# Sliding-window attention and two transformer layers: score products of the layers in blocks of 64 queries by 192 keys, a new order of steps, and a regrouped preparation of weights in the first stage

## The reference

```python
# attention: 16 heads of 64, windows of 64 keys
xn = x / max(norm(x), 1e-12) * 16 * gamma
q, k, v = split(xn @ W_qkv)
p = softmax(where(0 <= distance <= 64, q @ k.T / 8, -1e9))   # a block of 64 queries sees 128 keys
out = (p @ v) * sigmoid(xn @ W_gates + b_gates) @ W_out
# two layers: 8 heads of 64, windows of 128 keys
h = shift_token(x); q, k, v = split(h @ wqkv)
q, k = rotary_xpos(l2norm(q) * qs, l2norm(k) * ks)           # q is later scaled by 8
p = softmax(where(0 <= distance <= 128, q @ k.T, -max))      # a block of 128 queries sees 256 keys
x = x + (p @ v) @ wo
h = layernorm(shift_token(x)) * lg + lb
x = x + (a * gelu(g)) @ w2 + b2          # a, g = split(h @ w1 + b1)
```

## Time and profile before

| | before |
|---|---|
| median of 3 runs | 2063.93 us (2059.63 to 2064.92) |
| profiled execution | 2062.13 us, span 2060.3 us |
| PE / DVE / ACT / POOL busy | 92 / 64 / 68 / 47 % of the span |
| mean granted PE clock | 0.986 |

### The profile page before, as it was taken

How to read it: one execution, slowest core, us unless ns; L and a number is a source line. 1 busy time by engine, 2 the same in 40 slices (tenths; PEclk the granted TensorE clock), 3 DMA queues, 4 the chain that set the end, 5 groups by cost and what they waited for, 6 DMA issues and landing times.

```text
span 2060.3 us, 42560 instructions
## 1 busy us (share of the span) xinstructions
PE 1899.8 (92%) x15184; PEld 1575.3 (76%) x15184; DVE 1324.1 (64%) x4117; ACT 1400.8 (68%) x3933; POOL 959.0 (47%) x1311
## 2 busy tenths in 40 slices
PE   5999999999999789999999999997999999999998
PEld 3777787777777668778788787795877878878777
DVE  4543544444443467777778777775777877877775
ACT  4886977778678465775766757756576575675763
POOL 1532442334234463654736526545264562664732
PEclk9999999999999899999999999998999999999999
DMA  3231322313225411010110110304101011010110
GB/s 126 86 101 43 97 82 78 96 58 89 82 75 161 149 39 36 14 42 11 45 45 12 44 42 15 103 7 158 33 29 52 21 45 55 16 47 22 34 35 26
DMA packets 121493, 121.10 MB, mean 59 GB/s; under 512 B 27188, under 2 KB 100804, under 8 KB 121284
## 3 DMA queue, kind: packets, MB, share of 16 engines
q1 hardware_dynamic: 118116, 112.10, 17.0%
q10 hardware_dynamic: 3168, 6.29, 0.9%
HBM read 72.72 MB, written 37.25 MB: 53 GB/s over the span
## 4 chain that ended last, share of the span: by engine, by line
PE 32%; DVE 19%; ACT 9%; issue 2%; POOL 2%; SPq 1%; DMA 1%; DVEq 0%; ACTq 0%; POOLq 0%
PE f_bank L1352 11%; PE f_scores L1492 4%; ACT f_prob L1567 4%; PE f_scores L1430 4%; DVE f_u L1720 4%; PE f_bank L1478 4%; PE f_bank L1438 3%; DVE f_gu L1717 2%; PE f_o_bank L1453 2%; ACT f_u L1587 2%; DVE y_tok L1703 2%; PE f_bank L1403 2%; DVE y_tok L1709 1%; POOL f_prob L1305 1%; DVE f_sin_part L1623 1%
## 5 line engine op out<-in xcount | busy, mean ns | idle before, releaser
L1305 POOL TENSOR_SCALAR f_prob<-f_prob,f_row_inv 128x256 f32<-128x256 f32 x512 | 263.1, 533 | 331.0 <-DVE f_row_inv L1663 331.0
L568 POOL TENSOR_SCALAR a_prob<-a_prob,a_row_inv,a_gate 128x128 f32<-128x128 f32 x512 | 224.6, 455 | 409.8 <-DVE a_row_inv L898 409.8
L1352 PE MATMUL f_bank<-weights,f_actT 128*128 128x512 f32 x1152 | 305.6, 410 | 1.6 <-DVE f_actT L1606 1.6
L1478 PE MATMUL f_bank<-f_hT,f_w 128*128 128x256 f32 x2112 | 276.5, 286 | 7.7 <-DVE f_gu L1717 7.7
L1478 PEld LDWEIGHTS f_bank<-f_hT,f_w 128*128 128x128 f32 x2112 | 262.1, 190 | 14.3 <-DVE f_gu L1717 10.8
L1567 ACT ACTIVATE f_prob<-f_scores,f_neg_max 128x256 f32<-128x256 f32 x512 | 235.9, 488 | 41.8 <-DVE f_neg_max L1655 40.8
L1352 PEld LDWEIGHTS f_bank<-weights,f_actT 128*128 128x128 f32 x1152 | 211.2, 193 | 51.2 <-ACT f_probT L1514 5.1
L1281 POOL TENSOR_TENSOR f_norm<-f_norm,f_minus_half 128x16 f32<-128x16 f32 x64 | 197.5, 3085 | 24.8 <-DVE f_norm L1615 22.4
L1655 DVE CUSTOM_DVE_ANT_0 f_scores<-f_scores,f_mask 128x256 f32<-128x256 f32 x512 | 199.8, 455 | 13.5 <-PE f_scores L1430 13.4
L1587 ACT ACTIVATE f_u<-f_gu 128x256 fp32r<-128x256 f32 x192 | 80.2, 418 | 180.8 <-DVE f_gu L1717 180.8
L797 ACT ACTIVATE a_prob<-a_scores,a_neg_max 128x128 f32<-128x128 f32 x512 | 179.5, 390 | 30.2 <-DVE a_neg_max L889 28.9
(11 more groups left out here) (128 smaller groups left out, 3844.2 us busy)
## 6 DMA issues: line engine op xcount, KB each, us to landing
split_weights<-a_hi_lo SPq DMA_DIRECT2D x16, 512.0 KB, 2.8
x_next<-states SPq DMA_DIRECT2D x32, 256.0 KB, 3.1
tables<-scaled_tables SPq DMA_DIRECT2D x16, 512.0 KB, 6.0
f_x<-states SPq DMA_DIRECT2D x16, 512.0 KB, 5.2
split_weights<-a_hi_lo SPq DMA_DIRECT2D x12, 682.0 KB, 4.0
weights<-split_weights ACTq DMA_DIRECT2D x6, 1024.0 KB, 9.7
f_w<-split_weights SPq DMA_DIRECT2D x4, 1280.0 KB, 9.9
a_x_tok<-in_x SPq DMA_DIRECT2D x8, 512.0 KB, 4.4
```

Of the source, the lines that this page charges most:

```text
L568: last = nc.gpsimd.tensor_scalar(part, part, row_inv[:, a % 2, head, t:t + 1], gate[:, half, t, h:h + 1], ALU.mult, ALU.mult)
L1305: last = nc.gpsimd.tensor_scalar(part, part, row_inv[:, a % 2, head, t:t + 1], 1.0, ALU.mult, ALU.mult)
L1352: last = nc.tensor.matmul(out, lhs(c, a), rhs(c, b), start=(i == 0), stop=(i == len(order) - 1))
L1478: mm = nc.tensor.matmul(out[:, which * PART:(which + 1) * PART], w1[:, wp, c, col:col + P], hT[:, hp, c, columns_of(a // FH)], start=(i == ...
```

## The change

- The layers' score products take 64 queries by 192 keys instead of 128 by 256. Corners that no product writes are cleared once in PSUM. Since the masking then must not change sign, the sign goes into the query tables and the mask.
- `ORDER` is a new list. Among the changes: `transpose_x` stands ahead of the first `softmax`, `load_tables` ahead of `load_others`, `project_o` 1 behind `up` 0, `add_attended` right before `out` 0.
- First stage: x is loaded first; the pieces of weights are cut by groups of heads (both halves of the features in one piece), have a staging place each (the last one shares), and three of the nine splits stand in the first iteration's list `opening`. PE waits for each split only where it is used.
- The squares (`rms_sum`) go; the mean of squares after the norm is computed from the variance (two small DVE instructions). The scaled x goes to a tile of its own, so that `load_x` waits for the scaling and the store, no longer for the transposes.

The diff, cut to its core:

```diff
-        before = [("load_x", e), ("norm_stats", e), ("norm_apply", e), ("rms_sum", e), ("rms_scale", e), ("split", 0), ("rms_apply", e),
-                  ("split", 1), ("transpose_x", e), ("split", 2), ("split", 3), ("split", 4), ("gates", e), ("project_qk", a0), ("gates_back", e), ("split", 5),
-                  ("project_qk", a0 + 1), ("split", 6), ("project_qk", a0 + 2), ("split", 7), ("project_qk", a0 + 3), ("split", 8)]
+        before = [("load_x", e), ("norm_stats", e), ("rms_scale", e), ("norm_apply", e), ("split", 0), ("rms_apply", e), ("split", 1),
+                  ("transpose_x", e), ("split", 2), ("project_qk", a0), ("project_qk", a0 + 1), ("gates", e), ("split", 3), ("project_qk", a0 + 2),
+                  ("gates_back", e), ("split", 4), ("project_qk", a0 + 3), ("split", 5)]
+        opening = list(steps)
+        for n, step in ((6, ("softmax", 0)), (7, ("scores", 1)), (8, ("softmax", 2))):
+            opening.insert(opening.index(step) + 1, ("split", n))
...
+        stages = [raw[:], halves[:, 0], halves[:, 1], y_stage, table_stage, scaled_stage, late_q[:, 0], late_q[:, 1], y_stage]
+        pieces = [(w_gates.rearrange("(c p) n -> p c n", p=P), wgate, slice(0, A_HEADS))]
+        for group in range(A_GROUPS):
+            for n, (place, first) in enumerate(((wqk, 0), (wqk, A_INNER), (wv, 0))):
+                cols, place_cols = (slice(c0 + group * GC, c0 + (group + 1) * GC) for c0 in (n * A_INNER, first))
+                pieces.append((w_qkv[:, cols].rearrange("(c p) n -> p c n", p=P), place, place_cols))
...
+        SPLIT_OF_V, SPLIT_OF_QK, SPLIT_OF_OUT = (3, 6), (2, 7), (7, 8)
...
-                    sp.wait_ge(filled.sem, filled.past(it, ("transpose_x", h - 1), CT - 1) if h else filled.upto(it, -1))
+                    sp.wait_ge(x_ready.sem, x_ready.past(it, ("rms_apply", h - 1)) if h else x_ready.upto(it, -1))
+                    sp.wait_ge(normed_stored.sem, normed_stored.past(it, ("norm_apply", h - 1)) if h else normed_stored.upto(it, -1))
...
+            def load_piece(i):
+                sp.dma_start(stage_of(i), pieces[i][0]).then_inc(staged[i], 16)
+
             load_x(None, HALVES - 1)
-            for i, (src, _, _) in enumerate(pieces):
-                if i == 3:
-                    store_normed(None, HALVES - 1)
-                if i >= 3:
-                    sp.wait_ge(stage_emptied, i - 2)
-                sp.dma_start(stage_of(i), src).then_inc(staged[i % 3], 16)
+            sp.dma_start(ident[:], identity).then_inc(consts_loaded, 16)
+            sp.dma_start(gamma_row[:], gamma.unsqueeze(0).broadcast_to([P, D])).then_inc(consts_loaded, 16)
+            for i in (0, 1, 2):
+                load_piece(i)
+            sp.dma_start(bgate[:], b_gates.unsqueeze(1), allow_slow_non_contiguous=True).then_inc(consts_loaded, 16)
+            sp.dma_start(mask[:], masks.rearrange("s p k -> p s k")).then_inc(consts_loaded, 16)
+            for i in (3, 4):
+                load_piece(i)
+            store_normed(None, HALVES - 1)
+            for i in (5, 6, 7):
+                load_piece(i)
+            sp.wait_ge(stage_emptied, 4)
+            load_piece(8)
             sp.wait_ge(zero_rows_ready, 1)
             sp.dma_start(states[:, 0, :], zero_rows[:]).then_inc(zero_rows_stored, 16)
             sp.wait_ge(zero_rows_stored, 16)
-            sp.wait_ge(stage_emptied, len(pieces))
+            sp.wait_ge(stage_emptied, 1)
...
-            pe.wait_ge(stage_emptied, len(pieces))
...
+                    if a == a0:
+                        pe.wait_ge(stage_emptied, SPLIT_OF_QK[0] + 1)
+                    project_qk(None, a)
...
+                        if it == 0 and a == PAIRS:
+                            pe.wait_ge(stage_emptied, SPLIT_OF_QK[1] + 1)
...
-                    nc.scalar.activation(square[:], x_tok[:, t, :], ACT.Square, accum_out=sumsq[:, t:t + 1]).then_inc(squared.sem, 1)
...
-                dve.wait_ge(squared.sem, squared.past(it, ("rms_sum", h), TILES - 1))
-                nc.vector.tensor_scalar(rms[:], sumsq[:], 1e-24, 1.0 / D, ALU.max, ALU.mult).then_inc(ms_ready.sem, 1)
+                dve.wait_ge(var_ready.sem, var_ready.past(it, ("norm_stats", h)))
+                nc.vector.reciprocal(rms[:], spread[:]).then_inc(spread_inverted.sem, 1)
+                dve.wait_ge(spread_inverted.sem, spread_inverted.past(it, ("rms_scale", h)))
+                nc.vector.scalar_tensor_tensor(out=rms[:], in0=mean_var[:, :, 1], scalar=1e-24 / D * 1e-5, in1=rms[:], op0=ALU.max,
+                                               op1=ALU.mult).then_inc(ms_ready.sem, 1)
...
-                dve.wait_ge(normed_stored.sem, normed_stored.past(it, ("norm_apply", h)))
+                dve.wait_ge(x_normed.sem, x_normed.past(it, ("norm_apply", h)))
+                if it is not None:
+                    dve.wait_ge(filled.sem, filled.past(it, ("transpose_x", h - 1), CT - 1) if h else filled.upto(it, -1))
                 for t in range(TILES):
-                    last = nc.vector.scalar_tensor_tensor(out=x_tok[:, t, :], in0=x_tok[:, t, :], scalar=rms[:, t:t + 1], in1=gamma_row[:],
+                    last = nc.vector.scalar_tensor_tensor(out=x_scaled[:, t, :], in0=x_tok[:, t, :], scalar=rms[:, t:t + 1], in1=gamma_row[:],
...
-ORDER = [("scores", 0), ("scores", 1), ("softmax", 0), ("softmax", 1), ("weigh", 0), ("weigh", 1), ("transpose_x", 0), ("load_x", 0),
-         ("scores", 2), ("transpose", 0), ("softmax", 2), ("scores", 3), ("weigh", 2), ("weigh", 3), ("load_x1", 0), ("load_others", 0),
-         ("transpose", 1), ("softmax", 3), ("load_tables", 0), ("project_qk", 0), ("rope", 0), ("scores", 4), ("values", 0), ("values", 1),
-         ("take_o", 0), ("transpose", 2), ("project_qk", 1), ("softmax", 4), ("scores", 5), ("weigh", 4), ("transpose", 3), ("rope_sum", 0),
-         ("project_qk", 2), ("values", 2), ("softmax", 5), ("scores", 6), ("weigh", 5), ("values", 3), ("rope", 1), ("take_o", 1),
-         ("transpose", 4), ("scores", 7), ("softmax", 6), ("transpose_qk", 0), ("weigh", 6), ("project_qk", 3), ("shift_keys", 0),
-         ("project_o", 0), ("rope_sum", 1), ("weigh", 7), ("transpose", 5), ("values", 4), ("values", 5), ("softmax", 7), ("take_o", 2),
-         ("rope", 2), ("shift_front", 0), ("transpose", 6), ("project_v", 0), ("ln_stats", 0), ("transpose_qk", 1), ("transpose", 7),
-         ("ln_apply", 0), ("values", 6), ("values", 7), ("take_o", 3), ("project_v", 2), ("transpose_h", 0), ("project_o", 1), ("rope_sum", 2),
-         ("up", 0), ("shift_back", 0), ("up", 1), ("up", 2), ("ln_stats", 1), ("project_v", 1), ("ln_apply", 1), ("down", 0), ("project_v", 3),
-         ("up", 3), ("rope", 3), ("x1_bias", 0), ("down", 1), ("down", 2), ("transpose_h", 1), ("load_wqkv", 0), ("up", 4), ("up", 5),
-         ("down", 3), ("add_attended", 0), ("up", 6), ("up", 7), ("up", 8), ("up", 9), ("rope_sum", 3), ("down", 4), ("transpose_qk", 2),
-         ("down", 5), ("up", 10), ("down", 6), ("up", 11), ("down", 7), ("down", 8), ("transpose_qk", 3), ("out", 0), ("down", 9), ("down", 10),
-         ("down", 11), ("out", 1)]
+ORDER = [("scores", 0), ("transpose_x", 0), ("softmax", 0), ("scores", 1), ("weigh", 0), ("load_x1", 0), ("weigh", 1), ("softmax", 1),
+         ("scores", 2), ("transpose", 0), ("scores", 3), ("weigh", 2), ("softmax", 2), ("load_tables", 0), ("transpose", 1), ("softmax", 3),
+         ("values", 0), ("weigh", 3), ("project_qk", 0), ("values", 1), ("rope", 0), ("load_x", 0), ("scores", 4), ("take_o", 0),
+         ("transpose", 2), ("project_qk", 1), ("scores", 5), ("weigh", 4), ("softmax", 4), ("rope_sum", 0), ("load_others", 0), ("transpose", 3),
+         ("values", 2), ("scores", 6), ("weigh", 5), ("softmax", 5), ("project_qk", 2), ("rope", 1), ("values", 3), ("take_o", 1), ("scores", 7),
+         ("transpose", 4), ("softmax", 6), ("weigh", 6), ("project_qk", 3), ("project_o", 0), ("rope_sum", 1), ("weigh", 7), ("transpose", 5),
+         ("values", 4), ("softmax", 7), ("values", 5), ("take_o", 2), ("transpose", 6), ("project_v", 0), ("transpose_qk", 0),
+         ("shift_front", 0), ("values", 6), ("transpose", 7), ("ln_stats", 0), ("shift_keys", 0), ("ln_apply", 0), ("transpose_qk", 1),
+         ("rope", 2), ("transpose_h", 0), ("values", 7), ("take_o", 3), ("project_v", 2), ("rope_sum", 2), ("up", 0), ("project_o", 1),
+         ("up", 1), ("up", 2), ("project_v", 1), ("shift_back", 0), ("down", 0), ("down", 1), ("ln_stats", 1), ("ln_apply", 1), ("down", 2),
+         ("up", 3), ("project_v", 3), ("rope", 3), ("transpose_h", 1), ("up", 4), ("up", 5), ("down", 3), ("up", 6), ("x1_bias", 0), ("up", 7),
+         ("up", 8), ("down", 4), ("rope_sum", 3), ("down", 5), ("down", 6), ("load_wqkv", 0), ("transpose_qk", 2), ("up", 9), ("up", 10),
+         ("down", 7), ("up", 11), ("down", 8), ("down", 9), ("transpose_qk", 3), ("add_attended", 0), ("out", 0), ("down", 10), ("down", 11),
+         ("out", 1)]
...
```

(24 more changed lines are left out.)

125 lines of the change are left out of this document (65 added, 60 removed).

## The result

The change makes the kernel slower. Its median is 2072.5 us (2071.0 to 2075.3) against 2064.0 (2059.6 to 2064.9) of the kernel before: ratio 1.0047, 95% interval 1.0037 to 1.0057 (taken over the single runs; the two medians by themselves give 1.0041). The forecast was 2029, the upper end of its range 2052.

A forecast was written before the change was run, and what follows sets the result against it. PE, busy 1899.8 of 2060.3 us, was taken as the bound, except in chunk openings. Terms -12.8 - 13.3 - 7.4 - 2 + 0.9 = -34.6 us gave 2027.5, forecast as 2029 for the median; range 2000 to 2052.

The forecast's parts named there:

- Part 1: Layers' score products in 64 by 192 blocks: a step falls from 1.07 to 0.84 to 0.86 us, saving 27 us of PE.
- (c): Rival, layers' scores: quadrants don't overlap at 192 columns, 0.43 us a step more, 2095 us in all; chance 0.04.
- (d): Rival, layers' scores: more records cost time of their own and eat the 0.21 us a step, 2043 us; chance 0.03.
- Part 2: New order in each layer chunk: longer opening, shorter scores and fewer POOL waits give -0.8 us a chunk, -12.8 us in all.
- 0.5 us more: Chunk openings: the longer chain swallows the saving of its four score steps and costs this much more a chunk.
- Behind the opening PE is again the one that others follow: Rest of each chunk after the opening: PE sets the pace, so four shorter score steps save 0.85 us.
- -0.85 a chunk: Score steps behind each chunk's opening: four steps save 0.21 us each.
- -0.45: POOL's waits outside the openings: 0.5 us a chunk should nearly vanish, saving 0.45 us.
- Rival (b): Chunk openings: PE's granted clock falls behind the longer wait, +24 us, 2053 us in all; chance 0.10.
- Part 3: Weight reload between layers: tables issued ahead of the weights remove PE's 10.59 us stall and slow clock, -13.3 us.
- Part 4: Program start: x loaded first brings first scores at 33 us, 9.4 earlier; less 2 us for splits on ACT, -7.4 us.
- Part 5: Squares and the rest: removing ACT's squares gives -2 us, DVE's clears of four PSUM tiles cost +0.9 us.

The follow-up runs named there:

- e11: e3 with ten added identity transposes between scores 1 and 2 and five before each head's first transposes, holding the clock; 2046.3 us, ratio 0.9919.
- e4: The changed kernel with 24 unused identity transposes added between scores 1 and 2 of every chunk, holding the clock; 2060.1 us, ratio 0.9978.
- e3: The changed kernel with one step moved back: transpose_x behind softmax 1, as in the old list; 2053.6 us, ratio 0.9952.
- e13: The changed kernel with one small ACT exponential ahead of each chunk's two copies, so the table load comes early; 2072.7 us, ratio 1.0045.
- e5: The kernel before with ten identity transposes added between scores 1 and 2 and five before each head's first transposes, holding the clock; 2062.3 us, ratio 0.9993.
- e8: e6 with half of POOL's division in the layers left out; 2034.2 us, ratio 0.9856.
- e6: e1 with the same added transposes as e5, holding the clock; 2062.6 us, ratio 0.9993 against the kernel before.
- e14: e12 with the old scores, in blocks of 128 queries by 256 keys; 2046.1 us, ratio 0.9919.
- e1: The kernel before with only the 64 by 192 score blocks, the flipped sign and the clears; 2070.1 us, ratio 1.0038.
- e15: The kernel before with only the table loads moved ahead of the second layer's weights; 2051.6 us, ratio 0.9945.
- e9: The kernel before with only the change of the attention stage (first stage, squares included); 2063.5 us, ratio 1.0007.
- e12: e11 with splits 6 and 7 moved behind the division of unit 1; 2042.8 us, ratio 0.9898.
- e10: The changed kernel with splits 6 and 7 moved behind the division of unit 1; 2071.2 us, ratio 1.0043.
- e2: The kernel before with only the new ORDER, early tables included; 2084.2 us, ratio 1.0105.

## Why the prediction was wrong, step by step

- **Part 1, the step of scores: right.** 0.82 us predicted at 0.84 to 0.86; the quadrants overlap at 192 columns, and 16 records take no longer in turn than their columns, so rivals (c) and (d) are out.
- **Part 2, the opening's chain: right in its order, wrong in its price.** Copies, table load, exponentials and the wait of 3 us came as written. The price was "0.5 us more" for the opening; the move of x's transposes costs 0.86 us a chunk at full clock (e11 against e4) and 1.2 with the falls (e3). The reciprocal behind DVE's subtractions, which part 2 names, is a second chain to the division, and e13 shows that it ends only 0.6 us before the first.
- **The step that failed: "Behind the opening PE is again the one that others follow".** I had taken PE's unbroken work after the opening as proof that PE sets the pace. e5 to e8 show that POOL follows so closely that what PE saves becomes waiting for it. The -0.85 a chunk is 0 (e6 against e5) in the old order and about -0.25 in the new one (e14), and POOL's waits, which were to vanish (-0.45), doubled. The trace of before had the hint: 38 waits for POOL, 22 more than the openings have the earlier trace rows. It was read as small change, not as a second engine just behind the first.
- **Rival (b), the clock, was the one that came, at a chance of 0.10.** I gave it +24 us; it is 12.4 (e4), 0.2 to 0.4 us for each us at the lower level (e4 and e3) instead of the 0.5 that I had reckoned with. The likely reason is that half speed costs nothing where PE would have waited anyhow. The clock is one cause beside the failed step and the opening's price at full clock, not the whole. Part 1 has a share in the clock's loss that I did not see: shorter scores alone empty the opening enough for the clock to fall (e1), 7.4 us of loss (e1 against e6).
- **Part 3: right.** 13.3 predicted, 11.8 measured (e15), inside its bounds of 10.6 and 14.5.
- **Part 4: the mechanism of the first 35 us right (first scores at 35.0, forecast 33), the gain wrong.** -7.4 became 0 (e9, which holds part 5's squares too, so their -2 also came to nothing in the time). I charged the splits in the first iteration by ACT's time, 2 us of 0 to 4; their price was DVE, which works in program order and waits for ACT's half ahead of the masks. Moved behind the first divisions they give back 3.5 us (e12 against e11), and 1.3 in the changed kernel (e10), where that is within the noise.
- **Part 5.** The clears cost 2.1 us from 687.04, the wait for ACT's copies of v fell by 1.2 us, not 2.

The parts alone give +6.3 (e1), +20.4 (e2) and +0.2 us (e9), together 27 and not the 8.7 measured. They don't add. The loss to the clock stands in e1 and again in e2, and in the changed kernel once. And behind an opening that ends 3 us late PE may be the last one again, so that shorter scores help; that is only argued, and how the 18 us divide was not separated.

Set against the sum: of the 43 us between 2029 and 2072.5, parts 4 and 5 are some 10 and part 3 is 1.5. The rest is part 2, whose -12.8 came out as 8.7 + 11.8 - 0.2 = +20.3. It was made of +8 for the openings, -13.6 for the scores and -7.2 for POOL's waits. The runs give +13.8 for the place of x's transposes at full clock (e11 against e4) and +12.4 for the clock (e4). All else that is new in the layers, blocks included, is left with -5.9 where -20.8 was forecast. (The three are differences of runs taken in this order; in another order they can divide otherwise.) The largest error is thus the saving that didn't arrive, then the clock, then the price of the opening.

## What to carry to other kernels

An engine that hardly ever idles is not yet the bound: ask how far behind it the next engine stands, and price a saving by that slack, not by the work removed. Where the first engine waits at the head of every iteration, its shorter work only lengthens the wait, and a longer wait can cost the clock of what follows; try each reordering with the clock held before judging it. A step put on an engine that works in order costs what it waits for there too, not only what it runs.
